# Rows gathered per tile inside the looped experts, w1 loaded per tile by SyncE, and another routing chain

## Chip, cores and metric

One core of one Trainium2 chip. The time is device microseconds of one launch. The kernel computes one decoder layer for 32 sequences of 128 tokens with 128 features, all in float32. The change touches the third sub-layer (a mixture of 8 experts, one expert for each token) and the end of the second one.

## The reference, cut to what matters

```python
x = _layernorm(x + attention(x))                 # sub-layer 1
x = _layernorm(x + retention(x, ctx_1024))       # sub-layer 2
x = _layernorm(x + _L0_ffn_ref(x, Wg, bg, W1, b1, W2, b2))   # sub-layer 3
def _L0_ffn_ref(x, Wg, bg, W1, b1, W2, b2):      # 8 experts, D 128, hidden 512
    gate_scores = softmax(einsum('btd,de->bte', x, Wg) + bg)
    top1_idx = argmax(gate_scores)               # one expert for each token
    top1_mask = one_hot(top1_idx, 8)
    top1_weight = sum(gate_scores * top1_mask)
    h = silu(einsum('btd,edh->bteh', x, W1) + b1)
    o = einsum('bteh,ehd->bted', h, W2) + b2
    return sum(o * top1_mask) * top1_weight
```

Only the chosen expert's output counts. The kernel therefore sorts the 4096 tokens by expert, pads each expert's list to whole tiles of 128 tokens, and computes each tile with the weights of one expert. With 8 experts there are at most 32 + 7 = 39 tiles (NT), and all 39 are always computed.

## The kernel before

The kernel is written engine by engine: each phase is a block in which TensorE (PE), VectorE (DVE), ScalarE (ACT), GpSimd (POOL) and SyncE (SP) have instruction streams of their own, tied by semaphores. A block begins when all engines have finished the block before. An operation on tile t usually waits for a counter of the tile that used the same buffer before. Five blocks follow one another: attention_phase, retention_phase, gate_phase, expert_phase, finish_phase.

retention_phase (sub-layer 2, 8 groups of 4 sequences). Its first work on DVE is norm_dve (L129), a chain of small operations, after which DVE writes x1 (L1007) and PE transposes it (L918). PE transposes the context rows first (L912). POOL begins with a memset of a tile named padding (L880): 39 tiles of 128 rows with 129 columns, the last column holding a spare row number (L882). At its end SP loads the weights of the experts, w1 and w2, and the bias b2 into SBUF (preload, L871), and writes padding over the whole of a DRAM tensor sorted_x (L874). The block ends when these have landed (L875) and DVE has finished its last residual (L991) and statistics (L995).

gate_phase. norm_dve again, then 8 groups: DVE writes x2 (L1167), PE transposes it and multiplies with Wg (L1094, L1102), DVE adds bg (L1156), POOL copies x2 to x2_row (L1134). Then comes the routing chain, on DVE but for two matmuls and one exponential: maximum (L1181), softmax, the one-hot choice hot (L1202), for each expert the count of tokens before each token (two matmuls with constant matrices, L1109 and L1110, evacuated at L1206, and a prefix sum over the sequences in five doubling steps, L1213), the first tile of each expert, and for each token its row in the sorted order, place (L1247). Last, POOL scatters the tokens' rows to sorted_x: 32 indirect DMAs of 128 rows (L1142), each with 129 columns, the last one being the token's own number.

expert_phase, a loop over the 39 tiles. SP loads the sorted rows back into xs in four cuts (L1291). For tile t: ACT copies the rows to x_cur (L1367) and the expert's biases to b_cur (L1374), DVE copies the expert's part of w1 to w1_cur (L1410), PE transposes x_cur (turn, L1327), DVE evacuates it (evac, L1414), PE multiplies with w1_cur in four 128 x 128 x 128 products in two parts (L1343), ACT applies Silu with the bias (L1392), PE multiplies with w2 in four accumulating products (L1353) one tile behind, DVE adds b2 (L1433), and POOL scatters the 128 result rows to the DRAM tensor y_rows at the token's number (L1314), after casting the numbers (L1309) and a tiny addition (L1313) that carries a wait. run_steps (L83) peels the first steps and loops over pairs of tiles.

finish_phase. SP loads y_rows in token order in 8 groups (L1469), DVE and POOL scale with top and add x2_row (L1504, L1487, L1489), statistics, norm_dve, normalisation (L1461), and the stores.

## Time and profile before

| | before |
|---|---|
| time, median of 3 runs | 899.93 us (898.69 to 901.77) |
| time of the profiled execution | 903.15 us |
| its span, first to last instruction | 901.3 us |
| mean granted TensorE clock | 0.899 of full speed |

The stages of the span, from the times of instructions in the trace: attention to 601.8 us, retention to 684.8, gate and routing to 725.1, scatters of the rows to 766.5, experts from 771.0 to 869.6 (the last scatter of results starts at 863.8), finish to 901.3. The page's strip in 40 slices of 22.5 us, each digit a busy share in tenths, PEclk the granted clock in tenths:

```profile
PE   4789999999999999999999999748994600599920
DVE  4378788788788788878878878745885510244438
ACT  3677787788788778778778878321221100477720
POOL 2167667757757756766765775633431167266742
PEclk8799999999999999999999999967996555699975
```

Slices 33 and 34 (counted from 1) hold the scatters: TensorE stands still and GpSimd works. Section 5 of the page gives groups by line, section 6 the DMA issues with the time to landing; in the timelines the number in square brackets is the idle time of the engine just before the instruction and what ended it.

### The profile page before, as it was taken

The numbers are of one execution on the slowest core, as the hardware profiler recorded it, in microseconds if no ns is written. First come the engines' busy times: TensorE is split into PE (matmuls) and PEld (weight loads), VectorE is DVE, ScalarE is ACT, GpSimd is POOL, SyncE is SP. The second block draws the span as 40 slices with busy tenths as digits, with TensorE's granted clock in tenths as the row PEclk, the third lists the DMA queues.
The fourth block names the chain that finished last, engine by engine and source line by source line (L and its number), as shares of the span: only waits on it lengthen the run. The fifth ranks groups of instructions, "written<-read, shape, count | busy, mean of one in ns | idle before, by whom it ended". The sixth has DMA issues, their size and how long they took to land. (4 is left out here: it accounts for less than half of the span.)

```text
span 901.3 us, 26782 instructions
## 1 busy us (share of the span) xinstructions
PE 712.1 (79%) x9501; PEld 597.7 (66%) x9502; DVE 605.1 (67%) x1217; ACT 528.7 (59%) x1119; POOL 513.4 (57%) x524
## 2 busy tenths in 40 slices
PE   4789999999999999999999999748994600599920
PEld 3577788788778778778778877645664500598920
DVE  4378788788788788878878878745885510244438
ACT  3677787788788778778778878321221100477720
POOL 2167667757757756766765775633431167266742
PEclk8799999999999999999999999967996555699975
DMA  7567767767667677676776776611093011400033
GB/s 239 117 179 200 187 170 205 176 163 215 171 161 216 172 172 199 178 183 177 197 180 170 209 171 162 160 32 36 25 284 51 0 39 53 124 32 29 32 108 93
DMA packets 122154, 127.72 MB, mean 142 GB/s; under 512 B 7424, under 2 KB 101920, under 8 KB 118032
## 3 DMA queue, kind: packets, MB, share of 16 engines
q1 hardware_dynamic: 119584, 122.17, 52.8%
q0 software_dynamic: 2544, 5.21, 1.7%
q8 instruction: 15, 0.25, 0.1%
q14 instruction: 11, 0.09, 0.0%
HBM read 67.42 MB, written 43.16 MB: 123 GB/s over the span
## 5 line engine op out<-in xcount | busy, mean ns | idle before, releaser
L328 POOL TENSOR_TENSOR lhs<-pos_qv,ungate 64x1024 f32<-64x1024 f32 x64 | 151.7, 2370 | 161.9 <-PE mix L495 151.2
L614 ACT ACTIVATE psT<-bank 128x512 f32<-128x512 f32 x128 | 72.6, 594 | 92.5 <-PE bank L484 92.5
L766 DVE TENSOR_TENSOR lhs<-mix,zg_all 64x512 f32<-64x512 f32 x128 | 88.2, 689 | 5.8 <-PE mix L467 1.9
L353 POOL TENSOR_TENSOR e_qk<-e_qk 128x512 f32<-128x512 f32 (+2 forms) x96 | 78.6, 819 | 20.1 <-DVE e_qk L707 15.1
L484 PE MATMUL bank<-const,ps 128*128 128x128 f32 x512 | 70.0, 280 | 21.7 <-POOL ps L343 21.5
L598 ACT ACTIVATE e_qk<-e_qk 128x512 f32<-128x512 f32 x128 | 82.3, 643 | 0.0
L721 DVE TENSOR_REDUCE s_max<-bank 128x8 f32<-128x512 f32 x64 | 44.2, 691 | 48.7 <-PE bank L453 47.8
L467 PEld LDWEIGHTS mix<-pos_qv 64*64 64x64 f32 (+1 forms) x2048 | 65.6, 137 | 13.7 <-issue 11.2
L484 PEld LDWEIGHTS bank<-const,ps 128*128 128x128 f32 x512 | 55.2, 142 | 27.9 <-issue 15.7
L574 ACT ACTIVATE qk_tok<-bank 128x512 f32<-128x512 f32 x128 | 73.2, 601 | 0.0
L603 ACT ACTIVATE qkT<-bank 128x512 f32<-128x512 f32 x128 | 71.2, 610 | 1.8 <-PE bank L430 1.0
L467 PE MATMUL mix<-pos_qv 64*64 64x64 f32 (+1 forms) x2048 | 72.2, 225 | 0.0
L495 PE MATMUL mix<-psT,lhs 128*64 128x64 f32 x2048 | 69.7, 229 | 3.0 <-DVE lhs L766 2.2
L495 PEld LDWEIGHTS mix<-psT,lhs 128*64 128x64 f32 x2048 | 65.3, 143 | 8.6 <-issue 8.6
L389 PE MATMUL bank<-w_k,x_cur 128*128 128x512 f32 x192 | 63.6, 442 | 7.5 <-ACT psT L614 7.5
L430 PE MATMUL bank<-const,qk_tok 128*128 128x128 f32 x512 | 67.2, 273 | 2.7 <-DVE e_qk L707 2.1
L1410 DVE COPY w_cur<-w 128x512 f32 x39 | 16.8, 431 | 77.3 <-issue 48.6
L512 PE MATMUL bank<-w_o,attT 128*128 128x128 f32 x512 | 65.2, 282 | 4.0 <-DVE attT L700 4.0
L512 PEld LDWEIGHTS bank<-w_o,attT 128*128 128x128 f32 x512 | 61.0, 195 | 10.7 <-ACT qkT L603 7.1
L430 PEld LDWEIGHTS bank<-const,qk_tok 128*128 128x128 f32 x512 | 59.4, 140 | 12.8 <-DVE e_qk L707 2.5
L343 POOL TENSOR_TENSOR ps<-s_exp,row_rec 128x512 f32<-128x512 f32 x64 | 65.4, 1042 | 0.0
L336 POOL TENSOR_TENSOR ps<-pos_qv,sq_rec 128x1024 f32<-128x1024 f32 x32 | 60.9, 1902 | 5.9 <-POOL lhs L328 4.8
(212 smaller groups left out, 1694.5 us busy)
## 6 DMA issues: line engine op xcount, KB each, us to landing
scratch_qv<-qv_out SPq DMA_DIRECT2D x32, 1024.0 KB, 5.7
pos_qv<-scratch_qv SPq DMA_DIRECT2D x64, 512.0 KB, 6.6
swapT<-qkT SPq DMA_DIRECT2D x64, 256.0 KB, 4.0
zg_all<-scratch_z SPq DMA_DIRECT2D x64, 256.0 KB, 3.8
sorted_x<-padding SPq DMA_DIRECT2D x1, 2515.5 KB, 18.5
r_all<-in_x_dram SPq DMA_DIRECT2D x4, 512.0 KB, 7.0
cx<-in_ctx_dram SPq DMA_DIRECT2D x8, 256.0 KB, 2.7
w<-in_L_ffn_W_dram SPq DMA_DIRECT2D x1, 2048.0 KB, 9.7
```

The source lines that it names most:

```text
L328: pool.tensor_tensor(lhs[0:L, 1 - n, :, :], pos_qv[s, :, DK:], ungate[s, :, :], ALU.mult).then_inc(vg_ready, 1)
L353: pool.tensor_tensor(dst, e_qk[:, 0:c, DK:], e_qk[:, c:2 * c, DK:], ALU.add).then_inc(k_summed, 1)
L430: last = pe.transpose(qk_bank[f][:, i * P:(i + 1) * P], qk_tok[:, 4 * f + i, :], cst("ident"))
L467: last = pe.matmul(mix[odd * DK:(odd + 1) * DK, h // 8, at:at + DK], pos_qv[0:k, h, 0:DK], pos_qv[0:k, h, DK:], start=True, stop=True)
L484: last = pe.transpose(turn_bank[f % 2][:, i * P:(i + 1) * P], ps[:, 4 * f + i, :], cst("ident"))
L495: last = pe.matmul(mix[odd * DK:(odd + 1) * DK, n, at:at + L], lhs[:, 1 - n, h, :], psT[:, h, n * L:(n + 1) * L], start=True, stop=True)
L512: last = pe.matmul(score_bank[1][:, 0:D], attT[:, c, :], w_o[:, c, :], start=(c == 0), stop=(c == C // 2 - 1))
L574: act.activation(qk_tok[:, 8 * hh:8 * hh + 8, slot * DK:(slot + 1) * DK], half_bank(bank, hh), ACT.Copy).then_inc(evac, 1)
L598: act.activation(e, e, ACT.Exp, scale=-1.0).then_inc(grown, 1)
L603: act.activation(qkT[:, :, 4 * f:4 * f + 4], qk_bank[f][:, :].rearrange("p (c s) -> p s c", c=4), ACT.Copy).then_inc(qkT_evac, 1)
L614: act.activation(psT[:, 4 * f:4 * f + 4, :], turn_bank[f % 2][:, :].rearrange("p (h s) -> p h s", h=4), ACT.Copy).then_inc(psT_evac, 1)
L766: dve.tensor_tensor(dst, mix[odd * DK:(odd + 1) * DK, g, :].rearrange("p (i n k) -> p i n k", n=SEG, i=4), zg_all[odd * DK:(odd + 1) * DK, ...
```

## The change

- retention_phase: the padding tile, its memset and its write to DRAM are gone, and w1 is not preloaded.
- gate_phase: SP writes the rows x2_row to a DRAM tensor x2_rows in token order, a group at a time beside the loop. The one-hot choice comes from the logits, without the softmax; top is the reciprocal of the sum of exponentials. The counts are laid out expert by expert, and one tensor_tensor_scan replaces the doubling steps. place is still computed, but in place of 32 scatters the kernel inverts the list on the chip: DVE builds one-hot matrices in_row (which of 128 rows) and at_tile (which of 39 tiles), POOL and ACT scale at_tile with the sequence and the token number (in_tile), and PE adds up 32 products (list_bank), which gives for each tile and row the token it holds. DVE makes two lists of row numbers from it, token_of (where to read) and row_to (where to write).
- expert_phase: for each tile POOL gathers its 128 rows from x2_rows with an indirect DMA into one of four buffers xs, and scatters the results from y, which holds all 39 tiles, so both are written in one unrolled stream: six gathers, then a gather and a scatter in turn. SP loads the tile's w1 from DRAM into one of four buffers. ACT reads its bias straight from biases and makes no copies; DVE only evacuates PSUM (evac, keep). PE transposes the next tile between the two parts of the first product. run_fours peels four steps and loops over four.
- The finish phase is the same, and so is the attention phase. The constants grow by 289 columns.

The diff, cut to its core (the waits inside the routing chain are left out, and of removed code only what stands in a line's place):

```diff
+def run_fours(eng, step, n):
+
+    for t in range(4):
+        step(t, t, 0)
+    with eng.Fori(1, n // 4) as i:
+        for k in range(4):
+            step(4 * i + k, k, i)
+    for t in range(n - n % 4, n + 1):
+        step(t, t % 4, t // 4)
...
             for target, source in preload:
                 sp.dma_start(target, source).then_inc(preloaded, 16)
-            sp.wait_ge(padded, 2)
-            sp.dma_start(sorted_x.rearrange("(t p) d -> p t d", p=P), padding[:, :, :]).then_inc(preloaded, 16)
-            sp.wait_ge(preloaded, 16 * (len(preload) + 1))
+            sp.wait_ge(preloaded, 16 * len(preload))
 
         @block.gpsimd
         def _(pool):
-
-            pool.memset(padding[:, :, :], 0.0).then_inc(padded, 1)
-            pool.wait_ge(padded, 1)
-            pool.tensor_copy(padding[:, :, D:].rearrange("p t o -> p (t o)"), cst("spare_row")).then_inc(padded, 1)
...
+            for g in range(NG):
+                sp.wait_ge(x2_kept, g + 1)
+                sp.dma_start(x2_rows[G * g * P:(G * g + G) * P, :].rearrange("(b p) d -> p b d", p=P),
+                             x2_row[:, G * g:G * g + G, :]).then_inc(x2_stored, 16)
+            sp.wait_ge(x2_stored, 16 * NG)
...
-            flat = hot[:, :, :].rearrange("p b e -> p (b e)")
-            pe.matmul(rank_bank[:, 0, :, :].rearrange("p b e -> p (b e)"), cst("below"), flat, start=True, stop=True)
-            pe.matmul(rank_bank[:, 1, :, :].rearrange("p b e -> p (b e)"), cst("ones"), flat, start=True, stop=True).then_inc(ranked, 1)
+            pe.matmul(rank_bank[:, 1, :, :], cst("ones"), by_expert(hot[:, :, :]), start=True, stop=True)
+            pe.matmul(rank_bank[:, 0, :, :], cst("not_below"), by_expert(hot[:, :, :]), start=True, stop=True).then_inc(ranked, 1)
+            for b in range(B):
+                if b % G == 0:
+                    pe.wait_ge(in_row_ready, b // G + 1)
+                if b % (B // 2) == 0:
+                    pe.wait_ge(in_tile_ready, b // (B // 2) + 1)
+                    pe.wait_ge(token_ready, b // (B // 2) + 1)
+                last = pe.matmul(list_bank[:, 0:2 * NT], in_row[:, b, :], in_tile[:, b, :, :].rearrange("p o t -> p (o t)"), start=(b == 0), stop=(b == B - 1))
+            last.then_inc(listed, 1)
...
+            for i in range(2):
+                half_b = slice(i * B // 2, (i + 1) * B // 2)
+                act.wait_ge(placed, i + 1)
+                act.activation(in_tile[:, half_b, 1, :], at_tile[:, half_b, :], ACT.Copy, scale=cst("token")).then_inc(token_ready, 1)
...
-            pool.tensor_copy(x2_row[:, :, D:].rearrange("p b o -> p (b o)"), cst("token_row")).then_inc(x2_kept, 1)
-            pool.wait_ge(x2_kept, NG + 1)
-            pool.wait_ge(placed, 1)
-            for b in range(B):
-                pool.indirect_dma_start(sorted_x, bass.IndirectOffsetOnAxis(ap=place[:, b:b + 1], axis=0),
-                                        x2_row[:, b, :], None).then_inc(scattered, 16)
-            pool.wait_ge(scattered, 16 * B)
+            for i in range(2):
+                half_b = slice(i * B // 2, (i + 1) * B // 2)
+                dims = [P, B // 2, NT]
+                pool.wait_ge(placed, i + 1)
+                pool.tensor_tensor(in_tile[:, half_b, 0, :], at_tile[:, half_b, :],
+                                   cst("batch")[:, half_b].unsqueeze(2).to_broadcast(dims), ALU.mult).then_inc(in_tile_ready, 1)
...
+            dve.tensor_tensor(hot[:, :, :], logits[:, :, :], bc(top), ALU.is_equal).then_inc(done, 1)
+            dve.scalar_tensor_tensor(hot[:, :, :], hot[:, :, :], -float(E), iota, ALU.mult, ALU.add).then_inc(done, 1)
+            dve.tensor_reduce(index[:, :], hot[:, :, :], X, ALU.min).then_inc(done, 1)
+            dve.scalar_tensor_tensor(hot[:, :, :], iota, -float(E), bc(index), ALU.add, ALU.is_equal).then_inc(hot_ready, 1)
+            dve.tensor_tensor(logits[:, :, :], logits[:, :, :], bc(top), ALU.subtract).then_inc(shifted, 1)
+            dve.wait_ge(ranked, 1)
+            dve.tensor_tensor_scan(upto_batch[:, :, :].rearrange("p e b -> p (e b)"), cst("first"),
+                                   rank_bank[:, 1, :, :].rearrange("p e b -> p (e b)"), 0.0, ALU.mult, ALU.add).then_inc(done, 1)
+            last_of = upto_batch[:, :, B - 1:].rearrange("p e o -> p (e o)")
+            dve.tensor_scalar(padded[:, :], last_of, P - 1.0, None, ALU.add).then_inc(done, 1)
+            dve.tensor_tensor(row_of[:, :, :], upto_batch[:, :, :], rank_bank[:, 0, :, :], ALU.add).then_inc(done, 1)
+            dve.tensor_scalar(tiles[:, :], padded[:, :], WHOLE, None, ALU.bitwise_and).then_inc(done, 1)
+            dve.tensor_tensor_scan(tile_end[:, :], cst("ones")[:, 0:E], tiles[:, :], 0.0, ALU.mult, ALU.add).then_inc(done, 1)
+            dve.tensor_tensor(tile_start[:, :], tile_end[:, :], tiles[:, :], ALU.subtract).then_inc(done, 1)
+            dve.tensor_tensor(row_of[:, :, :], row_of[:, :, :], tile_start[:, :].unsqueeze(2).to_broadcast([P, E, B]),
+                              ALU.add).then_inc(done, 1)
+            dve.tensor_tensor(row_of[:, :, :], row_of[:, :, :], by_expert(hot[:, :, :]), ALU.mult).then_inc(done, 1)
+            dve.tensor_reduce(place_f[:, :], row_of[:, :, :].rearrange("p e b -> p b e"), X, ALU.add).then_inc(done, 1)
+            dve.tensor_copy(place[:, :], place_f[:, :]).then_inc(done, 1)
+            dve.tensor_scalar(tile_u[:, :], place[:, :], WHOLE, None, ALU.bitwise_and).then_inc(done, 1)
+            dve.tensor_scalar(row_u[:, :], place[:, :], P - 1, None, ALU.bitwise_and).then_inc(done, 1)
+            for g in range(NG):
+                if g % (NG // 2) == 0:
+                    s = slice(G * g, G * g + B // 2)
+                    dims = [P, B // 2, NT]
+                    dve.tensor_tensor(at_tile[:, s, :], cst("tile_at").unsqueeze(1).to_broadcast(dims),
+                                      tile_u[:, s].unsqueeze(2).to_broadcast(dims), ALU.is_equal).then_inc(placed, 1)
+                s = slice(G * g, G * g + G)
+                dve.tensor_tensor(in_row[:, s, :], cst("lane").unsqueeze(1).to_broadcast([P, G, P]),
+                                  row_u[:, s].unsqueeze(2).to_broadcast([P, G, P]), ALU.is_equal).then_inc(in_row_ready, 1)
+            dve.reciprocal(top[:, :], total[:, :])
...
+            dve.wait_ge(listed, 1)
+            dve.tensor_copy(token_at[:, :], list_bank[:, NT:2 * NT])
+            dve.tensor_scalar(empty[:, :], list_bank[:, 0:NT], 0.0, None, ALU.is_equal).then_inc(done, 1)
+            dve.scalar_tensor_tensor(token_at[:, :], list_bank[:, 0:NT], float(P), token_at[:, :], ALU.mult, ALU.add).then_inc(done, 1)
+            dve.scalar_tensor_tensor(empty[:, :], cst("spare_row"), float(P), empty[:, :], ALU.add, ALU.mult).then_inc(done, 1)
+            dve.tensor_scalar(token_of[:, :], token_at[:, :], -float(P), 0.0, ALU.add, ALU.max)
+            dve.scalar_tensor_tensor(row_to[:, :], token_at[:, :], -float(P), empty[:, :], ALU.add, ALU.add)
...
+                    e = expert_of(sp, t)
+                    if not is_step(t, 0, 1, 2, 3):
+                        sp.wait_ge(hid, 2 * (t - 3))
+                    sp.dma_start(w1_cur[k][:, :], W1[bass.ds(e, 1)].rearrange("o d h -> d (o h)")).then_inc(w1_loaded[k], 16)
+
+            run_fours(sp, step, NT)
...
+            def gather(t):
+                if t < NT:
+                    if t > 3:
+                        pool.wait_ge(turned, t - 3)
+                    pool.indirect_dma_start(xs[t % 4][:, :], None, x2_rows,
+                                            bass.IndirectOffsetOnAxis(ap=token_of[:, t:t + 1], axis=0)).then_inc(x_loaded[t % 4], 16)
+
+            def scatter(t):
+                pool.wait_ge(y_kept, t + 1)
+                pool.indirect_dma_start(y_rows, bass.IndirectOffsetOnAxis(ap=row_to[:, t:t + 1], axis=0),
+                                        y[:, t, :], None).then_inc(stored, 16)
+
+            for t in range(6):
+                gather(t)
+            for t in range(NT):
+                gather(t + 6)
+                scatter(t)
+            pool.wait_ge(stored, 16 * NT)
...
+                        if part == 0 and not is_step(t, NT - 1):
+                            turn(t + 1, (k + 1) % 4, i + (k + 1) // 4)
                 if two:
+                    if not is_step(t, 1, 2):
+                        pe.wait_ge(y_kept, u - 1)
                     pe.wait_ge(hid_done, FT * (u + 1))
-
-                    if not one:
...
+            def hidden(t, p, part, e):
+                act.wait_ge(hid, 2 * t + part + 1)
+                if part == 0 and not is_step(t, 0, 1):
+                    act.wait_ge(y_done, t - 1)
+                for f in range(FT // 2 * part, FT // 2 * (part + 1)):
+                    act.activation(hT[p][:, f, :], h_bank[p][part][:, f * P:(f + 1) * P], ACT.Silu,
+                                   bias=biases[:, bass.ds(e, 1), f:f + 1].rearrange("p o d -> p (o d)")).then_inc(hid_done, 1)
...
-                dve.tensor_copy(w1_cur[p][:, :], w1[:, bass.ds(e, 1), :].rearrange("p o d -> p (o d)")).then_inc(w1_staged, 1)
-
-            def evac(t, p):
-                dve.wait_ge(turned, t + 1)
                 dve.tensor_copy(xT[p][:, :], turn_bank[p][:, 0:P]).then_inc(xT_evac, 1)
 
-            stage_w1(0, 0)
+            def keep(u, q):
+                e = expert_of(dve, u)
+                dve.wait_ge(y_done, u + 1)
+                dve.tensor_tensor(y[:, bass.ds(u, 1), :].rearrange("p o d -> p (o d)"), y_bank[q][:, 0:D],
+                                  biases[:, bass.ds(e, 1), FT:].rearrange("p o d -> p (o d)"), ALU.add).then_inc(y_kept, 1)
...
+        x2_rows = nc.dram_tensor("x2_rows", (B * P, D), F32, kind="Internal").ap()
...
-        preload = ((w1[:, :, :], W1.rearrange("e d h -> d e h")),
-                   (w2[:, :, :, :], W2.rearrange("e (f p) d -> p e f d", p=P)),
+        tile_expert, token_of, row_to = (ctx.enter_context(nc.sbuf_tensor(n, [P, NT], U32)) for n in ("tile_expert", "token_of", "row_to"))
```

## Rows read from the trace of the kernel before

**Rows 1.** Busy time in two stretches: PE, PEld, DVE, ACT, POOL, PEclk, DMA share, GB/s

```profile
580.00:590.00 10.00, 5.80 (x101) 5.15 (x99) 7.70 (x14) 3.17 (x6) 8.60 (x5) 1.00 0.18 53
...
800.00:820.00 20.00, 19.10 (x165) 18.46 (x164) 8.34 (x28) 15.40 (x57) 13.68 (x30) 1.00 0.10 33
```

**Rows 2.** Timeline of GpSimd: start, length, what, idle time before

```profile
726.02 1.08 POOL L1142 DMA_INDIRECT sorted_x<-x_row,place  x1 [19.91 <-DVE place L1247]
...
765.57 0.97 POOL L1142 DMA_INDIRECT sorted_x<-x_row,place  x1 [0.30 <-issue]
...
782.74 0.99 POOL L1314 DMA_INDIRECT y_rows<-y,row  x1 [0.48 <-issue]
...
847.39 0.99 POOL L1314 DMA_INDIRECT y_rows<-y,row  x1 [0.19 <-issue]
...
863.80 0.99 POOL L1314 DMA_INDIRECT y_rows<-y,row  x1 [0.15 <-issue]
```

**Rows 3.** Indirect DMAs: issues with us to landing, and the results' lengths in ns

```profile
y_rows<-y,row POOLq DMA_INDIRECT x39, 2.3
...
sorted_x<-x_row,place POOLq DMA_INDIRECT x32, 2.3
...
L1314 POOL DMA_INDIRECT y_rows<-y,row x39: 989/993/1252, 782.7 to 863.8; - x39
```

**Rows 4.** Timeline of the start of the retention phase, all engines

```profile
601.82 4.29 POOL L880 MEMSET padding<- 128x5031 f32 x1 [12.47 <-POOLq L176]
...
601.86 0.22 DVE L137 TENSOR_TENSOR r_mean<-stats 128x32 f32<-128x32 f32 x1 [0.31 <-PEq L176]
...
602.36 3.78 DVE L141 TENSOR_SCALAR r_mean<-r_mean 128x32 f32<-128x32 f32 x1
...
606.21 1.11 PE L912 MATMUL r_cxt<-const,cx 128*128 128x128 f32 x4 [5.32 <-DMA cx<-in_ctx_dram]
...
609.60 1.12 PE L918 MATMUL r_x1t<-const,x 128*128 128x128 f32 x4 [2.27 <-DVE x L1007]
```

**Rows 5.** End of the retention phase: the last DMA's landing, DVE's next start

```profile
sorted_x<-padding SPq DMA_DIRECT2D x1, 2515.5 KB, 18.5
...
684.90 0.21 DVE L137 TENSOR_TENSOR g_mean<-stats 128x32 f32<-128x32 f32 x1 [4.30 <-PEq L816]
```

**Rows 6.** Timeline of DVE in the routing chain: first, after the matmuls, last

```profile
710.39 0.42 DVE L1181 TENSOR_REDUCE top<-logits 128x32 f32<-128x256 f32 x1
...
717.80 0.42 DVE L1206 COPY count<-rank_bank 128x256 f32<-128x256 f32 x1 [2.17 <-PE rank_bank L1110]
...
724.96 0.18 DVE L1247 CAST place<-place_f 128x32 uint32<-128x32 f32 x1
```

**Rows 7.** Prices: DVE and GpSimd on 128x512, PE's gate products at low clock

```profile
679.00 0.69 DVE L991 TENSOR_TENSOR r_all<-r_out,r_all 128x512 f32<-128x512 f32 x1 [1.25 <-PE r_out L950]
...
875.02 1.11 POOL L1487 TENSOR_TENSOR y_tok<-y_tok,top 128x512 f32<-128x512 f32 x1 [10.22 <-DMA y_tok<-y_rows]
...
706.71 3.42 PE L1102 MATMUL g_logit<-wg,x2T 128*128 128x8 f32 x16
```

**Rows 8.** DVE in the finish phase, beside GpSimd's addition and alone

```profile
874.63 2.89 DVE L1504 SCALAR_TENSOR_TENSOR r_all<-y_tok,top,x_row 128x128 f32<-128x128 f32 x4
...
881.94 1.12 DVE L1504 SCALAR_TENSOR_TENSOR r_all<-y_tok,top,x_row 128x128 f32<-128x128 f32 x4
```

**Rows 9.** Timeline of PE in the experts: first transpose, one tile, two tiles on

```profile
774.03 0.48 PE L1327 MATMUL e_turn<-const,e_x 128*128 128x128 f32 x1 [56.27 <-ACT e_x L1367]
...
848.35 1.06 PE L1343 MATMUL h_bank_b<-e_xT,w_cur 128*128 128x128 f32 x8
...
852.62 1.06 PE L1343 MATMUL h_bank_b<-e_xT,w_cur 128*128 128x128 f32 x8
```

**Rows 10.** A plain load issued by GpSimd, and a 256 KB load's time to landing

```profile
3.62 0.58 POOL L310 DMA_DIRECT2D ungate<-in_L_attn_betas_dram  x1
...
cx<-in_ctx_dram SPq DMA_DIRECT2D x8, 256.0 KB, 2.7
```

283 lines of the change are left out of this document (95 added, 188 removed).

## The prediction

> **What bounds the kernel now.** I read the strip of 40 slices first: attention and retention keep PE at 9 tenths, the change hardly touches them, and behind them lie 220 us in which no engine is full for long. Then the timelines of GpSimd and PE there. GpSimd issues 32 scatters back to back; one takes 0.97 us and starts 0.30 us after the one before, 1.27 us each, from 726.02 to 765.57 [rows 2, 3]. PE has stood idle for 56 us when it makes its first transpose of the experts at 774.03 [rows 9]. So the path runs through DVE's routing chain, then through GpSimd's 32 descriptor lists, then through a landing and the load of the first tiles. In the experts two tiles take 852.62 - 848.35 = 4.27 us, 2.13 us each [rows 9], with PE busy 19.1 of 20 us at full clock [rows 1]: PE is the bound, with about 0.1 us of waiting in a tile, so a tile costs PE some 2.03 us. GpSimd has one scatter a tile and slack. The last scatter starts at 863.80 [rows 2]. What follows it is the same code before and after, so I forecast the start of the last scatter and carry its shift to the end.
>
> **Retention phase.** (a) Padding's memset holds GpSimd for 4.29 us, and beside it a DVE instruction on 32 columns takes 3.78 us where its neighbour needs about 0.2 [rows 4]. Without the memset DVE's norm chain is 3.6 us earlier. That chain ends in x1, for which PE waits until 609.60; the context transposes ahead of it on PE are bound by a DMA and end at 606.21 + 1.11 = 607.32. So PE is late next, and I count 609.60 - 607.32 = 2.3 us, not 3.6. (b) The write of padding takes 18.5 us to land, and DVE has been idle 4.30 us when the next block lets it go [rows 5]; a change of block with no DMA to wait for left DVE idle 0.31 us [rows 4]. Gain 4.0 us. The cover here is DVE's residual: the weights' loads were issued ahead of padding and have 2 MB less to bring, so they land before it. Together 6.3 us; the bounds are 4.0 (if x1 is held by something else) and 7.6.
>
> **Gate phase, the loop.** Eight writes of x2_rows on an idle SP queue, waiting for GpSimd's copy; nobody else queues behind them. A 256 KB load lands in 2.7 us [rows 10], the routing chain that follows is longer. Nothing.
>
> **Routing chain.** It begins at 710.39 and ends at 725.14, and a 128x256 operation takes 0.42 us, some 0.46 with its wait; a 32-column one 0.18 [rows 6]. From its beginning, in the new order: five operations to the one-hot choice, 2.3; rank matmuls 2.2 as before [rows 6], 4.5 so far. The scan isn't in the trace: between one pass of 128x256 (0.42) and two (0.9), I take 0.6. Then three 128x256 steps and seven small ones: 2.7, so 7.8. One-hot matrices: in_row is eight operations of 128x512 at 0.69, about 0.62 overlapped [rows 7], at_tile two of 624 columns at 0.8: 6.6, so 14.4. GpSimd's in_tile is two operations of 624 columns, 1.11 x 624 / 512 = 1.35 us each [rows 7]. In the finish phase four DVE operations with two SBUF inputs take 2.89 us beside such a GpSimd operation and 1.12 alone [rows 8]: 1.77 us lost to 1.11 us of GpSimd's work and more. in_row has two SBUF inputs as well, so I let GpSimd's two operations hold DVE up for their length: 2.7, so 17.1. PE's 32 products follow in_row; at low clock a product with its weight load costs 3.42 / 16 = 0.21 us [rows 7], four are left after the last in_row. DVE meanwhile has the sum, the reciprocal, after, expert_f and its cast: 1.9, so 19.0, then six small steps for the two lists, 1.1, and the change of block, 0.3 [rows 4]: 20.4 us. So the chain alone gets 5.6 us longer, not shorter (bounds 17 and 24: no hold-up and a cheap scan, or operations on broadcast and strided operands a third dearer). The experts' block begins at 710.39 - 6.3 + 20.4 = 724.5.
>
> The Trainium skill ("SBUF — State Buffer", section "Who interferes with whom") states that a DVE instruction with two SBUF inputs contends with a GpSimd instruction that reads SBUF, and that the one that comes second waits for the whole of the first. Rows 8 agree; without that rule the sum would be 2.7 us less.
>
> **Start of the experts.** GpSimd needs 0.9 us from release to its first indirect DMA (place ends at 725.14, 726.02 is the start [rows 2, 6]): 725.4. Landing 2.3 us later [rows 3]: the first transpose at 727.7. From the first transpose to the first scatter it took 782.74 - 774.03 = 8.7 us [rows 2, 9], at low clock for the most part; the same here, 736.4. Six gathers (7.7 us) and the seventh fit ahead of it. w1 of tile 0 is issued by SP at the block's start and lands in 2.7 us [rows 10], before xT is there. Bounds: 2 us either way.
>
> **The loop.** Per tile GpSimd now issues a gather and a scatter. The trace has no gather, and no indirect DMA that waits for nothing but a satisfied semaphore. Nearest rows: 0.99 us for a scatter in the loop, 0.30 us between two [rows 2]. I take 1.29 for both kinds, so 2.58 us a tile. PE's 2.03 us and w1's 2.7 us to landing, four buffers deep [rows 10], both fit under it: **GpSimd becomes the bound**, the experts go from 2.13 to 2.58 us a tile. From the first scatter to the start of the last there are 38 scatters and 32 gathers (tiles 7 to 38) to go: 70 x 1.29 = 90.3 us. The last scatter starts at 736.4 + 90.3 = **826.7**, against 863.80: 37.1 us earlier. The end has no further wait: after the last gather six scatters stand (7.7 us), about what the last tile needs from landing to result.
>
> Bounds on the price. Below: a plain load issued by GpSimd takes 0.58 us [rows 10]; were a gather 0.58 + 0.30, the loop would lose 32 x 0.41 = 13 us more. Above: where GpSimd has waited, a scatter starts 0.48 us after the instruction ahead of it, and where it hasn't, 0.15 to 0.19 [rows 2]. If each wait, satisfied or not, cost that difference on top (0.33), the price is 1.6 us and the loop 22 us longer. The short gaps in a loop that has waits as well speak for 1.29.
>
> Some scatters of the loop took up to 1.25 us against a median of 0.99 [rows 3]; these lie beside DVE's copy of w1, which is gone. The Trainium skill (the same page, section "A bandwidth-pool intuition that's wrong (but worth ruling out)") says that a copy from SBUF to SBUF on DVE locks GpSimd out of writing descriptors. By the rule every indirect DMA now takes 0.99; were it something else that goes on, half of them at 1.25 would make the loop 9 us longer.
>
> **The sum.** -6.3 (retention), +5.6 (chain), the rest from the scatters that are gone and the slower loop: -37.1 us in all. The profiled span of 901.3 would become 864.2, its execution 866.0; the median of the runs, 3.2 us below that execution, 899.93 - 37.1 = **862.8**.
>
> **The rivals.**
> - Forecast (0.68): GpSimd bound at 1.29 per indirect DMA, 855 to 872.
> - Dear waits (0.13): 1.6 per indirect DMA or slowed ones as above, 872 to 886. Speaks for it: each new DMA has a wait; against: the short gaps.
> - Cheap gathers (0.12): 849.8. PE's 2.03 us a tile is then nearly the bound. For: nothing of the row is written to DRAM; against: the list of 128 addresses is as long as a scatter's.
> - Slower than before, a gather that holds GpSimd until its rows have landed (0.03): 2.3 + 0.3 = 2.6 us each [rows 3], 32 x 1.31 = 42 us more, 904.7. It decides from 1.29 + 37.1 / 32 = 2.45 us a gather. Against: no scatter did so.
> - TensorE's clock stays at its lower level (1.2 GHz) because PE now pauses in each tile (0.02): 39 x 4.06 = 158 us from 727.7, the last scatter near 887, 923. It decides from 3.4 us a tile. Against: PE at 58% busy was granted 1.00 [rows 1], and at half clock PE has no pauses, being slower than GpSimd.
> - The change doesn't do what it says, some stage of the new chain costs 10 us or more (0.02): 873 and up, still faster.
>
> **Range and chances.** 8 in 10 from 849.5 (cheap gathers) to 883 (most of the dear waits). This kernel's measurement can tell some 0.3%, 2.7 us, from no change. Faster 0.94, within 0.3% 0.02, slower 0.04.
>
> **What would show it.** Right: in the new profile GpSimd's indirect DMAs follow each other without a gap of over 0.4 us from about 736 on, PE waits once a tile for a gather, DVE's norm chain in retention has no instruction of 3.8 us, the block before the gates ends with DVE. Wrong: scatters or gathers far from 0.99, PE without gaps, a hold of GpSimd by landings, the first gather before 720 or after 730.

## The result, and the profile of the changed kernel

| | before | after |
|---|---|---|
| median of 12 runs of each | 900.85 us | 891.41 us (886.86 to 897.60) |
| ratio, 95% interval | | 0.990 (0.9878 to 0.9921) |
| profiled span | 901.3 us | 892.7 us |
| first indirect DMA of the rows | 726.02 | 725.03 |
| last scatter of results | 863.80 | 851.02 |

The changed kernel is 1.0% faster. The forecast was 862.8 us with a range from 849.5 to 883.0: the sign was right, the size was not, and the time lies outside the range. Up to the first scatter nearly everything came as worked out. First DVE's rows that answer to [rows 4 to 6]: start, length, line and operation, and in brackets the idle time before and what ended it.

```profile
603.03 0.18 DVE L154 TENSOR_SCALAR r_mean<-r_mean 128x32 f32<-128x32 f32 x1
...
678.54 0.21 DVE L150 TENSOR_TENSOR g_mean<-stats 128x32 f32<-128x32 f32 x1 [0.31 <-PEq L829]
...
704.14 0.42 DVE L1212 TENSOR_REDUCE top<-logits 128x32 f32<-128x256 f32 x1
...
708.69 0.69 DVE L1225 TENSOR_TENSOR_SCAN upto_batch<-const,rank_bank 128x256 f32<-128x256 f32 x1 [1.96 <-PE rank_bank L1130]
...
713.40 3.52 DVE L1257 TENSOR_TENSOR in_row<-const,row_u 128x512 fp32r<-128x512 f32 x4
...
723.86 0.19 DVE L1277 SCALAR_TENSOR_TENSOR row_to<-token_at,empty 128x39 uint32<-128x39 f32 x1
```

The instruction of 3.78 us now takes 0.18, the block before the gates ends with DVE (idle 0.31 us, not 4.30), and the routing chain begins at 704.14, as forecast. Then GpSimd's timeline, against [rows 2], where each indirect DMA (L1332 gathers, L1337 scatters) now stands for one of 78.

```profile
725.03 1.09 POOL L1332 DMA_INDIRECT xs<-x_rows,token_of  x1 [5.69 <-POOLq L1044]
726.43 0.97 POOL L1332 DMA_INDIRECT xs<-x_rows,token_of  x1 [0.31 <-issue]
...
735.74 1.00 POOL L1337 DMA_INDIRECT y_rows<-y,row_to  x1 [2.04 <-DVE y L1415]
...
742.34 0.99 POOL L1337 DMA_INDIRECT y_rows<-y,row_to  x1 [1.74 <-DVE y L1415]
743.64 0.98 POOL L1332 DMA_INDIRECT xs<-x_rows,token_of  x1 [0.30 <-issue]
744.93 0.99 POOL L1337 DMA_INDIRECT y_rows<-y,row_to  x1 [0.30 <-issue]
746.22 0.98 POOL L1332 DMA_INDIRECT xs<-x_rows,token_of  x1 [0.30 <-issue]
748.87 0.98 POOL L1337 DMA_INDIRECT y_rows<-y,row_to  x1 [1.68 <-DVE y L1415]
...
851.02 0.97 POOL L1337 DMA_INDIRECT y_rows<-y,row_to  x1 [0.37 <-DVE y L1415]
```

The price of an indirect DMA is the forecast one, 0.98 + 0.30 = 1.28 us, but after every fourth GpSimd stands still for some 1.7 us, 1.4 more than the usual gap, waiting for DVE's addition y. From the first to the last scatter pass 115.3 us where the forecast had 90.3. The waits of this stretch by engine (us in total, times, longest), and the moment in which one of them ends, from the timeline:

```profile
POOL y_rows L1337 <- DVE y L1415: 32.7, 22, 2.1
...
745.62 1.06 PE L1379 MATMUL y_bank<-w,hT 128*128 x8
...
748.25 1.14 ACT L1393 ACTIVATE hT<-h_bank_a,biases 128x128 f32<-128x128 f32 x4 [3.79 <-remote]
748.30 0.29 DVE L1415 TENSOR_TENSOR y<-y_bank,biases 128x128 f32 x1 [4.62 <-remote]
748.51 0.28 DVE L1410 COPY e_xT<-e_turn 128x128 f32<-128x128 f32 x1
748.85 0.71 PE L1369 MATMUL h_bank_b<-e_xT,w_cur 128*128 128x128 f32 x4 [2.17 <-DVE e_xT L1410]
```

This is the place to read. DVE, ACT and PE are all idle, and start within 0.6 us of each other. "remote" means that the profile found no record of a releaser at that time. In the single records the product that DVE waits for (tile 4's y) ends at 744.59 and DVE's addition starts at 748.30, 3.7 us later; in the kernel before the same distance is 0.13 us on the mean and 0.19 at most. Below this distance is called **the lag**: the start of DVE's addition of b2 less the recorded end of the last product of its tile, over 39 tiles. In the changed kernel it is 2.29 us on the mean and 3.78 at most. Every late counter that I found is one that PE raises: of the 185 changes of ACT's and DVE's counters that this loop's trace holds none is more than 0.012 us behind its instruction. From DVE's addition to GpSimd's scatter behind it, where GpSimd waits, it is 0.28 us throughout.

The attention phase is the same in all kernels here, yet its end lies between 597 and 605 us in their profiled executions. Single times are therefore compared from the first indirect DMA of the experts to the end: 167.6 us in the changed kernel.

### The profile page after: what moved, and what is told of

Same layout as the page of the kernel before. It is cut to its first block and busy times, and to the rows that moved or that the text cites. A ratio compares the mean times of both kernels' runs of the same rounds, so it can differ in the third digit from the quotient of the medians.

```text
span 892.7 us, 26716 instructions
## 1 busy us (share of the span) xinstructions
PE 727.8 (82%) x9532; PEld 612.7 (69%) x9533; DVE 591.0 (66%) x1179; ACT 512.1 (57%) x1042; POOL 500.6 (56%) x451
## 5 line engine op out<-in xcount | busy, mean ns | idle before, releaser
L1415 DVE TENSOR_TENSOR y<-y_bank,biases 128x128 f32 (+1 forms) x39 | 11.4, 291 | 90.4 <-PE y_bank L1379 39.2
L402 PE MATMUL bank<-w_k,x_cur 128*128 128x512 f32 x192 | 61.8, 431 | 7.5 <-ACT psT L627 7.5
L402 PE MATMUL bank<-w_v,x_cur 128*128 128x512 f32 x192 | 60.1, 423 | 5.3 <-DVE w_v L691 3.4
```

What stands on the lines that cost most here:

```text
L402: last = pe.matmul(bank[hh][:, :], x_cur[p][:, x_at, :], w[:, w_at, hh * BANK:(hh + 1) * BANK], start=(i == 0), stop=(i == 2))
```

## The experiments

| kernel | time | first indirect DMA to end | first to last scatter | lag, mean / max |
|---|---|---|---|---|
| changed | 891.41 | 167.6 | 115.3 | 2.29 / 3.78 |
| w1_four | 886.51 | 164.6 | 112.2 | 1.69 / 3.87 |
| w1_copy | 892.56 | 168.6 | 116.5 | 1.85 / 3.35 |
| pool_on_dve | 891.24 | 167.6 | 115.3 | 2.40 / 3.78 |
| gather_four | 845.37 | 122.4 | 73.0 | 0.25 / 0.34 |
| dense_scatters | 897.97 | 175.3 | 121.5 | 2.55 / 3.80 |
| dense_gathers2 | 938.29 | 216.3 | (behind) | 4.33 / 41.1 |
| scatters_behind | 903.05 | 173.6 | (behind) | 2.00 / 34.6 |
| late_scatters | 885.16 | 163.9 | 106.2 | 2.23 / 5.91 |
| padded, padded2 | 893.12, 897.33 | 170.6, 171.2 | 118.0, 118.8 | 1.20, 1.64 / 2.77, 3.92 |
| scatter_third | 890.60 | 166.7 | 114.9 | 1.69 / 28.0 |
| scatter_second | 891.27 | 165.4 | 112.3 | 1.58 / 21.0 |
| spaced (1.80 us) | 906.15 | 180.2 | 125.8 | 0.26 / 0.44 |
| spaced_300 (1.51 us) | 891.37 | 165.6 | 112.7 | 2.13 / 4.49 |
| spaced_130 (1.37 us) | 888.91 | 167.3 | 114.7 | 1.96 / 3.83 |
| one_block | 882.23 | 160.5 | 115.3 | 2.42 / 3.81 |
| y_gathered | 870.94 | 147.6 | (none) | 0.27 / 0.63 |

The changed kernel ran 12 times, scatter_third and y_gathered four times, every other kernel once; the last three columns are from one profiled execution of each. (behind) means that the scatters stand behind the gathers.

### Which part of the loop makes PE's counters late?

**w1_four**: SP loads w1 for the first four tiles only, and waits for nothing; the later tiles compute with these old weights.

```diff
-                if not is_step(t, NT):
+                if is_step(t, 0, 1, 2, 3):
                     e = expert_of(sp, t)
```

> The changed kernel with w1 loaded by SP for tiles 0 to 3 only; the later tiles reuse those four buffers, so the experts' weights are left out for them. In the changed kernel the counter of y (raised by PE at the end of L1379) is seen up to 3.5 us after the last product's end, in every second tile, and GpSimd waits 1.4 us for VectorE each two tiles: 115.3 us from the first scatter to the last where 70 x 1.29 = 90 was forecast. Theory A, the w1 loads (256 KB a tile on SP's queue, and SP's waits) hold up PE's counters: the lag is gone, the stretch falls to 90 to 93 us, the kernel to about 867. Theory B, GpSimd's dense stream of gathers and scatters, or its wait for a counter of PE, does it: no change, 112 to 118 us. Theory C, the gathers' transfers do it: no change.

**w1_copy**: w1 is preloaded into SBUF and DVE copies it into the four buffers, as the kernel before did for two; the gathers stay.

> The w1 part undone alone: w1 preloaded in the retention phase and copied by VectorE for each tile into one of four buffers, SP idle in the experts; gathers and scatters as in the changed kernel. Theory A: no lag, 70 x 1.29 us plus up to a quarter of a microsecond for those indirect DMAs that meet VectorE's copy, 91 to 100 us from first to last scatter, the kernel 867 to 877. Theories B and C: lag as before, 112 to 122 us, the kernel 889 to 899.

**pool_on_dve**: the gather waits for DVE's evacuation, not for PE's transpose.

```diff
-                        pool.wait_ge(turned, t - 3)
+                        pool.wait_ge(xT_evac, t - 3)
```

> The changed kernel, with GpSimd's gather waiting for VectorE's evacuation counter (xT_evac) in place of PE's transpose counter (turned), as safe and a fraction of a microsecond later. GpSimd then waits for no counter of PE, as in the kernel before. Theory B in the form that a wait of GpSimd on PE's counter holds the counters up: the lag is gone, first to last scatter about 91 us, the kernel about 867. Theories A and C: no change, 112 to 118 us.

**gather_four**: only the first four tiles are gathered, so the rest computes on old rows.

```diff
-                if t < NT:
-                    if t > 3:
-                        pool.wait_ge(turned, t - 3)
+                if t < 4:
```

> The changed kernel with gathers for tiles 0 to 3 only; later tiles reuse those rows, so their own rows are left out. One indirect DMA a tile is left. Theory A (w1 loads): the lag of PE's counter stays, tiles at over 2.5 us, the stretch 95 us or more. Theories B and C (dense stream, or the gathers' transfers): no lag, PE bound at 2.0 to 2.1 us a tile, the stretch 76 to 80 us.

The w1 loads cost 3 us, DVE's copy in their place 1 us more than they do, the wait on PE nothing, each by one execution. Without the gathers the lag is gone: a tile takes 73.0 / 38 = 1.92 us, and PE is the bound, as it was before. So it is the gathers: their kind, or the stream that they make of GpSimd's work?

**dense_scatters**: gather_four (so the later tiles compute on old rows) with a second scatter of each tile, into a spare tensor. **dense_gathers2**: each gather twice, the second into a spare buffer, all scatters behind the last gather. **scatters_behind**: one gather a tile, all scatters behind the last.

```diff
                 scatter(t)
+                spare(t)          # dense_scatters; dense_gathers2: gather(t), spare(t)
```

> Rows are gathered for the first four tiles only, and each tile's y is stored twice, the second time into a spare tensor: GpSimd writes two indirect DMAs a tile as in the changed kernel, all of them scatters. If it is the dense stream of indirect DMAs on GpSimd that delays the counters, of whichever kind they are (theory B), keep comes some 2 us after y's end on the mean, as in the changed kernel (2.29), and first to last scatter lasts over 105 us. If it needs the gathers, their transfers into SBUF or their mixture with scatters (theory C), keep follows y by 0.25 us as with four gathers, and the stretch is GpSimd's own sum, 38 x 2 x 1.28 = 97 us, with the last spare scatter behind it. The output is the reference's only for the first four tiles' rows, since the others work on those tiles' x.

> Each tile's rows are gathered twice, the second time into a spare buffer, and all 39 scatters stand behind the last gather: during the loop GpSimd writes two indirect DMAs a tile, all gathers. Theory B (any dense stream): keep comes some 2 us after y's end on the mean while the gathers run, and the gathers' stretch is lengthened over its own sum of 38 x 2 x 1.28 = 97 us, to 105 or more. A theory that needs scatters in the stream: keep follows y by 0.25 us, and the gathers take 97 us. Behind them 39 scatters in one go, 39 x 1.28 = 50 us, so the whole is near 727 + 97 + 50 + 40 = 914 us or above in either case.

> One gather a tile, and all 39 scatters behind the last gather. Theory B: a stream with one indirect DMA per 1.9 us is not dense, so keep follows y by 0.3 us while the gathers run; the 35 gathers behind the first four go at PE's 1.92 us a tile (the pace with four gathers), 67 us, then 39 scatters at 1.28 us, 50 us, of which only the first wait for nothing: last scatter at about 727 + 67 + 50 = 844 us, 7 us before the changed kernel's 851, and a total of about 884 us. Theory C, a single gather's transfer is enough: keep comes over 1 us after y's end, and a tile takes over 2.3 us during the gathers.

Scatters alone and gathers alone do it as well; theory C (a gather's transfer) falls. One gather per 1.9 us doesn't: in scatters_behind, while the gathers ran, the tiles came every 1.95 us, PE was busy 14.94 to 15.00 of 15 us, and GpSimd's gathers were 0.95 us long with 0.94 us of waiting for PE between them. Its total was 903, not 884: there the price comes at the end, below. In dense_gathers2 GpSimd's timeline shows the largest hold. 14 gathers stand back to back from 720.15; the 15th waits for the transpose of tile 3, which PE's record puts at 731.80:

```profile
736.63 0.95 POOL L1343 DMA_INDIRECT spare_x<-x_rows,token_of  x1 [0.30 <-issue]
740.24 0.95 POOL L1333 DMA_INDIRECT xs<-x_rows,token_of  x1 [2.67 <-remote]
```

The counter was seen at 739.98, 7.8 us after the transpose's end, while the DMAs themselves did not fall behind: as far as their landings are recorded, the last record of each lies 2.2 to 3.2 us after its issue, 2.9 for the first of the 14 and 2.5 for the last. The load on the DMA engines isn't it either: their mean busy share was 0.40 in the changed kernel (800 to 820 us), and 0.70 in y_gathered below (740 to 780 us), where the lag is 0.27 us on the mean.

### What is the rule? A backlog of 1.43 us an indirect DMA

The runs so far gave the size. PE's held counters come out in bunches, the last bunch at a moment that follows from how many indirect DMAs stood in a row. The trace records when some counters changed; some examples, for rows of n, back to back from a start s to this release r:

```
n    kernel            s        r       (r - s) / n
1    scatter_third     773.68   775.14  1.46
2    scatter_third     770.53   773.38  1.42
4    changed           742.34   748.05  1.43
4    changed           755.33   761.03  1.42
7    changed           725.03   734.92  1.41
14   dense_gathers2    720.15   739.89  1.41
24   scatter_third     802.78   836.86  1.42
38   dense_gathers2    833.06   886.47  1.41
```

These aren't picked for their fit. All kernels here but before, spaced and spaced_300 together have 155 rows of four (no kernel's last row counted); behind 149 of them a counter came over 0.25 us late, and for 142 of these (r - s) / n lies between 1.38 and 1.48. Not all held counters wait for the end of the row: in dense_gathers2 and late_scatters most rows of four let one out after 2.8 us, about 2 x 1.41, and in the row of 38 single ones came out up to 50 us before the last.

**Theory D**: behind GpSimd each indirect DMA of 128 rows is worked off in about 1.43 us. GpSimd issues one in 1.28, so in a row a backlog grows, and while there is one PE's counters can be held. What is worked off isn't the transfer: in the kernel before 32 scatters in a row at 1.27 us each landed 2.3 to 2.8 us after their start, the last after 2.34 [rows 2, 3]. In the changed kernel this makes a circle: a row of four from 742.34 is worked off at 742.34 + 4 x 1.43 = 748.06, then the counters come, DVE adds (748.30 to 748.59), GpSimd's next scatter starts at 748.87, 0.8 us after the release. Two tiles take 5.7 + 0.8 = 6.5 us, where the forecast had 4 x 1.29 = 5.2.

**late_scatters**: the scatter of tile t - 3 behind the gather of tile t + 6.

```diff
-            for t in range(NT):
+            for t in range(NT + 3):
                 gather(t + 6)
-                scatter(t)
+                if t > 2:
+                    scatter(t - 3)
```

> The scatter of tile t-3 stands behind the gather of tile t+6, where the changed kernel has the scatter of tile t: GpSimd waits for y that was kept three tiles earlier. If the delay of the counters has a bound of some 3.5 us whatever the stream does, GpSimd never waits, the stretch is near 38 x 2 x 1.28 + 3 x 1.28 = 97 us less the last three, and the total falls by some 20 us to about 868 us. If the counters are only seen when GpSimd idles (the other form of theory B: the stream itself holds them back and its end releases them), the delay grows until GpSimd stands still again, and the stretch stays at 110 us or more, the total within 5 us of the changed kernel's.

9 us shorter from scatter to scatter, but these begin 5.5 us later, so 4 us from the first indirect DMA on: neither form's number. The waits for y fell to 7.3 us, but 23.9 us of waits stand at the gathers now, which wait for a counter of PE as well. More slack moves the stall; the hold grew (5.91 us).

**padded** and **padded2**: one or two memsets of a column behind each indirect DMA.

> A memset of one column behind each indirect DMA: GpSimd's period per indirect DMA grows from 1.28 us to something near 1.5 us. Theory D (something behind GpSimd takes 1.42 us for each indirect DMA, as 14 of them in 19.9 us in the run with doubled gathers and 4 in 5.7 us in the changed kernel suggest, and PE's counters are held back while it has a backlog): no backlog arises, keep follows y by under 0.5 us on the mean, GpSimd's waits for y nearly vanish, and first to last scatter lasts 38 x 2 x its period, 111 to 115 us at 1.46 to 1.52 us. The rival (the counters are late whenever GpSimd works without a longer pause, at whatever rate): keep still comes over 1.5 us after y, and the stalls stay on top of the pads: over 122 us.

> Two such memsets behind each indirect DMA, a period near 1.65 us. Theory D: no backlog, keep within 0.3 us of y's end, the stretch 38 x 2 x 1.65 = 125 us. The rival: keep over 1.5 us after y and a stretch over 130 us.

Neither tested the theory. The period stayed 1.28 us, as the memset vanished in the gap of 0.30 (yet the stretch from scatter to scatter grew by 2.7 and 3.5 us, unexplained), here two lines of padded:

```profile
752.74 0.98 POOL L1333 DMA_INDIRECT xs<-x_rows,token_of  x1 [0.19 <-issue]
753.72 0.11 POOL L1346 MEMSET spare_col<- 128x1 f32 x1
```

**scatter_third** and **scatter_second**: in the gathers' part a scatter for every third or second tile, the others behind the last gather.

```diff
+            for t in range(6, NT):
+                gather(t)
+                if t % 3 == 0:      # scatter_second: t % 2
+                    scatter(sent)
+                    sent += 1
+            for t in range(sent, NT):
+                scatter(t)
```

> One gather a tile and one scatter for every three tiles; the 28 other scatters stand behind the last gather. PE sets the pace of the gathers with 1.92 us a tile, so GpSimd has 4 indirect DMAs in 5.8 us, 1.44 us each. Theory D: just above the 1.42 us at which a backlog would grow, so keep follows y by under 0.6 us on the mean during the gathers, the last gather starts near 725 + 9 + 33 x 1.92 = 797 us, and the 28 scatters behind it take 36 us: last scatter near 835 us against 851, a total near 876 us, 15 us below the changed kernel's. The rival (dense work of any rate): one scatter in three already brings keep over 1 us behind y, the gathers take over 2.3 us a tile and the total is 885 us or more.

> One scatter for every two tiles: 3 indirect DMAs per two tiles, 1.28 us each at PE's 1.92 us a tile, which is GpSimd's own rate. Theory D: a backlog grows and is waited out, so the pace is 3 x 1.42 / 2 = 2.13 us a tile, keep over 1 us behind y on the mean; 33 gathers take 70 us, 22 scatters behind them 28 us: last scatter near 832 us. The rival (no such bound): keep follows y by 0.3 us and a tile takes 1.92 us, last scatter near 826 us.

Both missed their totals. In scatter_second a tile took 2.49 us (tiles 4 to 34), not theory D's 2.13, and in scatter_third 2.28, not 1.92: the pair of a scatter and a gather holds the counters until 1.6 us after the second's start, and the single gather behind it for 1.4. The larger loss is the end. The last gather and 23 of the 28 scatters behind it, 24 indirect DMAs in a row from 802.78, hold back PE, which still has the last tiles to compute:

```profile
832.03 0.97 POOL L1337 DMA_INDIRECT y_rows<-y,row_to  x1 [0.30 <-issue]
837.68 0.97 POOL L1337 DMA_INDIRECT y_rows<-y,row_to  x1 [4.69 <-DVE y L1420]
```

802.78 + 24 x 1.43 = 837.1; DVE's addition starts at 837.11. In scatters_behind 36 in a row from 799.16 give 799.16 + 36 x 1.43 = 850.6, and the next scatter starts at 851.22. The last one starts at 859.12, where 844 was expected: most of the 19 us that it lost.

**spaced**, **spaced_300**, **spaced_130**: a memset of 640, 300 or 130 columns behind each indirect DMA, long enough to set the period.

```diff
+                pool.memset(spare_cols[:, :], 0.0).then_inc(paused, 1)
```

> A memset of 128x640 stands behind each indirect DMA. A memset of one or two columns vanished in the 0.30 us between two indirect DMAs, so this one is meant to bring their period to 1.5 to 1.7 us. Theory D (each indirect DMA is worked off in 1.44 us behind GpSimd, and PE's counters may be held until nothing is left; releases at the last start + 1.44, 1.6, 1.92 and 3.62 us for 1, 2, 4 and 14 in a row speak for it): nothing piles up, a counter is held by one indirect DMA at the most, under 1.44 us, keep follows y by under 0.7 us on the mean and 1.5 us at the most, and the stretch from first to last scatter is 38 x 2 periods, 114 us at 1.5, without waits for y. The rival (PE's counters wait for a pause of GpSimd, whatever its rate): keep still comes over 1.5 us behind y, and the waits stay on top of the longer period: over 135 us.

> The memset behind each indirect DMA is cut to 300 columns. 640 columns took 0.66 us and the next indirect DMA began 0.16 us later, so 300 should give a period of 0.98 + 0.37 + 0.16 = 1.51 us, a little over theory D's 1.44. It says: each indirect DMA is worked off before the next begins, a counter is held 1.44 us at the most, keep follows y by under 0.9 us on the mean, GpSimd waits for y little, and the stretch is near 38 x 2 x 1.51 = 115 us. If the bound lies higher, between 1.51 and 1.80, the releases stay bunched, keep comes over 1.5 us behind y, and the stretch is over 122 us.

> 130 columns: a period of 0.98 + 0.22 + 0.16 = 1.36 us, under 1.44. Theory D: the backlog grows by 0.08 us with each indirect DMA and holds TensorE's counters until GpSimd stands still: keep over 1.5 us behind y on the mean, bursts that end in waits for y as in the changed kernel, a stretch of 115 us or more (the burst of four is worked off at 4 x 1.44 from its start, whatever the period). If the bound is below 1.36, keep follows y by 0.3 us and the stretch is 38 x 2 x 1.36 = 103 us.

At 1.80 us GpSimd never rests for longer than 0.2 us, and yet the lag is 0.26 us and 0.44 at most: it isn't GpSimd's work without a pause, it is the rate of indirect DMAs. At 1.37 the kernel behaves as at 1.28. At 1.51 theory D as stated was wrong: the lag was 2.13 us, where it had allowed 0.9, though the stretch of 112.7 us was near its 115.

```profile
752.81 0.98 POOL L1334 DMA_INDIRECT xs<-x_rows,token_of  x1 [0.16 <-issue]
753.78 0.66 POOL L1346 MEMSET spare_cols<- 128x640 f32 x1
...
745.73 0.98 POOL L1334 DMA_INDIRECT xs<-x_rows,token_of  x1 [0.16 <-issue]
746.70 0.37 POOL L1346 MEMSET spare_cols<- 128x300 f32 x1
747.94 0.98 POOL L1339 DMA_INDIRECT y_rows<-y,row_to  x1 [0.86 <-DVE y L1429]
```

(The first two lines are of spaced, the others of spaced_300.) The records of counters in spaced_300 suggest why. Between 750.8 and 755.5 PE's counters are seen at 750.87, 752.37, 753.08, 753.86 and 755.40; but for the third, each lies 1.38 to 1.43 us after the start of an indirect DMA and 0.1 us ahead of the next. So the 1.4 us stand, but it looks as if the 0.1 us left over lets one counter through, and PE raises four in a tile while GpSimd leaves two such gaps. The rest piles up until GpSimd waits for something. No run tests this reading.

Theory D is also not the whole rule. A lone DMA mostly holds nothing: in spaced no recorded counter of PE is over 0.2 us late, and in gather_four, scatters_behind and y_gathered one of 103 lone DMAs had a counter over 0.25 us late behind it. In scatter_third, where they stand among pairs, it was 12 of 22. When a lone one holds, and where between 1.51 and 1.80 us the lag ends, stays open.

### A version that follows from it

**one_block**, a control: experts and finish in one block, all adds of the finish on DVE. **y_gathered**: in the same block, and without scatters. SP stores each tile's y in the tiles' order, 32 gathers bring the tokens' rows back behind the experts, and DVE's adds and statistics run beside them.

```diff
+                sp.dma_start(y_rows[bass.ds(u, 1)]..., y[:, bass.ds(u, 1), :]...).then_inc(stored, 16)
...
+            for b in range(B):
+                pool.indirect_dma_start(y_tok[:, b, :], None, y_rows.rearrange("t p d -> (t p) d"),
+                    bass.IndirectOffsetOnAxis(ap=place[:, b:b + 1], axis=0)).then_inc(y_loaded[b // G], 16)
```

> The changed kernel with its experts and its finish in one block, and all adds of the finish on VectorE: a control for the next run. In the changed kernel 8.1 us lie between the end of the last scatter (852.0) and the first load of y_tok (860.1), of which some 2 us are the scatter's landing; without the change of blocks about 6 us go, VectorE's extra adds cost 0 to 4 us: about 887 us. Theory D: the loop's stretch stays at 115 us.

> No scatters: SyncE stores each tile's y in the order of the tiles, and 32 gathers bring the tokens' rows back behind the experts, in one block with the finish, whose adds and statistics run beside them. Theory D: with one gather for 1.92 us beside the experts nothing piles up, keep follows y by 0.3 us, the experts go at PE's pace and the last y is kept near 728 + 39 x 1.92 + 3 = 806 us; its store lands by 809, 32 gathers at 1.28 us end at 850, the norm chain and the rest take 16 to 18 us: a span of about 868 and a total near 870 us, 21 below the changed kernel, 17 below one_block. The rival (any indirect gather beside PE delays it, and the run with four gathers was quick for another reason): over 2.3 us a tile, and a total over 885 us.

y_gathered takes 870.94 us (868.49 to 876.75), 0.967 of before (0.960 to 0.973), and beats both kernels. Of the 20.0 us that it is shorter than the changed kernel from the first indirect DMA on, 7.2 come with the single block (one_block), 12.8 with the gathers. GpSimd and DVE in it:

```profile
792.06 0.95 POOL L1363 DMA_INDIRECT xs<-x_rows,token_of  x1 [1.27 <-PE e_turn L1382]
...
807.04 0.29 DVE L1445 TENSOR_TENSOR y<-y_bank,biases 128x128 f32<-128x128 f32 x1 [1.08 <-PE y_bank L1408]
...
809.93 0.95 POOL L1370 DMA_INDIRECT y_tok<-y_rows,place  x1 [14.99 <-DMA y_rows<-y]
...
848.85 0.95 POOL L1370 DMA_INDIRECT y_tok<-y_rows,place  x1 [0.30 <-issue]
```

The last y was forecast for 806, the end of the gathers for 850. The 32 gathers in a row hold nobody back, as PE has nothing left to do.

## Why the prediction was wrong, step by step

| step | forecast | measured |
|---|---|---|
| routing chain begins | 704.1 | 704.14 |
| first gather | 725.4 | 725.03 |
| first transpose, first scatter | 727.7, 736.4 | 727.97, 735.74 |
| one indirect DMA | 1.29 | 1.28 |
| 70 of them, first to last scatter | 90.3 | 115.3 |
| last scatter | 826.7 | 851.02 |
| last scatter to the end | 37.5 | 41.6 |

**Retention.** Forecast gain 6.3 us; the start of the phase to the routing chain went from 108.5 to 101.6 us, 6.9. Both causes were right, and so was the choice of 2.3 us for the norm chain.

**Routing chain.** 20.4 us forecast with the change of block; row_to ends 19.9 us after the chain's beginning. The scan took 0.69 us (0.6 forecast), in_row 0.88 us an operation where 0.62 and 2.7 us of hold-up for eight made 0.96. That it got longer, not shorter, was right. Six of the eight took 0.68 us, and the two that began beside a GpSimd operation 1.72, until 0.5 us after its end: 2.1 us of hold-up. The trace agrees with the rule of the Trainium skill ("SBUF — State Buffer", section "Who interferes with whom") on two SBUF inputs.

**Start of the experts.** Within 0.7 us.

**The loop: the step that failed.** The sentence was "I take 1.29 for both kinds, so 2.58 us a tile", and from it 70 x 1.29. The price was right; that GpSimd would work without gaps was not. The sum took the time in which GpSimd issues a DMA for the whole of what it costs, and held PE at 2.03 us a tile for covered. The runs showed a second cost, some 1.43 us per indirect DMA in which PE's counters can be held, and GpSimd's scatter waits in a circle for just these. Of the 22 waits for y, 32.7 us in all, 0.3 us each is the usual gap and 1.7 us of the first lie ahead of the stretch: 24.4 of the 25.0 us. Only 20.7 of these are waits for held counters: the last five waits, 3.7 us without the usual gaps, come behind the last gather (seven scatters stand there, not six), where the lag is 0.16 to 0.26 us and PE, which the holds had put behind, sets the pace. No rival named this: "dear waits" had the right size (up to 22 us) with another mechanism, a price of each wait, and the short gaps of 0.30 within each row of four rule it out. The catch-all of 0.02 ("some stage of the new chain costs 10 us or more") covers the time and names no mechanism. It isn't the clock either: PE's granted clock was 1.00 from 800 to 820 us, with PE busy 12.7 of the 20. The rows of before could not show the effect: its 32 scatters in a row have no PE beside them [rows 2], and in its loop the scatters are 2.1 us apart on the mean (one 1.6, the others 1.9 and more), wider than the 1.80 at which spaced has no lag either. What could have been seen is that no row had PE working beside a dense stream of indirect DMAs. That is a resource the trace didn't show, and it got no bound.

**The end.** "The same code before and after" was the second miss, 4.1 us. From the last scatter to the first load of y_tok it took 5.9 us before, now 9.1, here before and after:

```profile
869.70 5.30 SPq L1469 DMA_DIRECT2D y_tok<-y_rows  x8
...
860.12 5.58 SPq L1460 DMA_DIRECT2D y_tok<-y_rows  x8
```

These 3.2 us are GpSimd's DRAIN at the end of the block, 3.2 us long before and 6.4 after; the other 0.9 us are not accounted for. With one block the distance is 2.3 us. The drain goes with the number of indirect DMAs in the block, 0.082 us for each: 3.2 us with 39, 3.6 with 43 (gather_four), 6.4 with 78, 6.7 with 82 (dense_scatters). With 117 (dense_gathers2) it took only 3.8, so this is no rule for larger numbers. What the drain waits for was not tried.

**Copy and descriptors.** The slow scatters of 1.25 us [rows 3] are gone, and the reason that I gave fits. In the kernel before 16 of the 39 scatters began 0.05 to 0.26 us behind the start of DVE's copy of w1. Each of them ended 0.87 us after the end of the copy, and so took 1.04 to 1.25 us; the 23 others took 0.99. The longest one:

```profile
849.70 0.43 DVE L1410 COPY w_cur<-w 128x512 f32 x1 [0.75 <-PE h_bank_b L1343]
849.75 1.25 POOL L1314 DMA_INDIRECT y_rows<-y,row  x1 [0.46 <-DMA y_rows<-y,row]
```

This agrees with the rule of the Trainium skill ("SBUF — State Buffer", section "A bandwidth-pool intuition that's wrong (but worth ruling out)") by which such a copy locks GpSimd out of writing descriptors. Only the first 0.1 us of the scatter seem to count: 16 copies of the kernel before began 0.1 to 0.7 us into a scatter, took their 0.43 us, and left the scatter at 0.99. In w1_copy, where DVE copies w1 again, no copy that began ahead of an indirect DMA was still running 0.1 us into it, so that kernel doesn't test the rule.

**Sum.** 37.1 us forecast, 8.6 in the spans. The 28.5 missing are, but for rounding, 25.0 (loop) and 4.1 (end), less 0.7 for the earlier first scatter.

## To carry to other kernels

Before an engine is made the bound by giving it a stream of small DMAs, look for a row in which the other engines work beside such a stream; if there is none, leave room in the range. Where several engines go idle together and start within a few tenths of a microsecond, while the product they wait for ended long before by the records, count what the DMA-issuing engine did in between. Put dense indirect DMAs where no one waits for TensorE, and beside it keep them 1.8 us or more apart, the shortest period without a lag here (1.51 was too short).

## What the runs showed of the hardware

- Counters that TensorE raises can be seen late beside indirect DMAs issued by GpSimd: by a lag of up to 3.8 us in the changed kernel, 7.8 us behind 14 in a row, 41 us behind 38. In the examples above, rows of 1 to 38, the last of them come 1.41 to 1.46 us per DMA (128 rows of 512 bytes) after the row began, and in the changed kernel's rows of four this bunch comes within 0.3 us.
- Not every counter in a row is held; in the first 7 us of the row from 725.03 the transposes were evacuated 0.5 us after their start.
- A memset of up to 0.15 us between two indirect DMAs fits into their gap of 0.30 us, and the period stays 1.28 us (padded, padded2).
- A scatter that begins 0.05 to 0.26 us behind a copy on DVE (128 x 512, float32, SBUF to SBUF) ends 0.87 us after the copy instead of 0.99 us after its own start (kernel before).
- GpSimd's drain at the end of a block took 0.082 us for each of its 39 to 82 indirect DMAs, and 3.8 us in all with 117.
- What carries out the hold stays open. The Trainium skill ("Perfetto Trace Analysis", section "Tensor Engine Instruction (MATMUL, LD_WEIGHTS)") says that the end of a matmul in the profile is worked out, and that its counter goes out when PSUM has acknowledged the write. Either the acknowledgement or the counter's way may be what waits; no run here tells these apart.
